# A two-layer transformer on one core: the quantised feed-forward spread over both attentions

## What is computed

```python
x = x + L0_attn(L0_cond(x))          # "layer 0": adapter matmul, 32 small heads
x = x + L0_ffn(L0_cond2(x))          # routed low-rank feed-forward
x = x + L1_attn(L1_cond(x))          # "first attention": 32 heads of 128, 8 kv heads
x = x + L1_ffn(L1_cond2(x))          # "second attention" over 512 cached + 128 own keys,
                                     # then the quantised feed-forward

def _fake_quant_lastdim(x):
    s = jnp.maximum(jnp.max(jnp.abs(x), axis=-1, keepdims=True) / 127.0, 1e-08)
    return jnp.clip(jnp.round(x / s), -127.0, 127.0) * s
def _dyn_quant_linear(x, w, b):
    return jnp.einsum('bti,oi->bto', _fake_quant_lastdim(x), _fake_quant_lastdim(w)) + b
h = _layernorm(vit_embeds, gamma, beta)      # vit_embeds: output of the second attention
h = _dyn_quant_linear(h, w1, b1)             # w1, w3: 512 x 512
h = jax.nn.gelu(h, approximate=False)
h = _dyn_quant_linear(h, w3, b3)
```

## Time and profile before

| | us |
|---|---|
| median of 3 runs (2221.23 to 2223.15) | 2221.28 |
| profiled execution, its own time | 2225.66 |
| its span, first to last instruction | 2223.6 |
| scores of item 60 start at | 2032.69 |
| PE busy | 2057.3 |
| DVE busy | 1564.7 |
| ACT busy | 1304.6 |
| POOL busy | 793.9 |

### The profile page before, as it was taken

How to read it: one execution, slowest core, us unless ns; L and a number is a source line. 1 busy time by engine, 2 the same in 40 slices (tenths; PEclk the granted TensorE clock), 3 DMA queues, 4 the chain that set the end, 5 groups by cost and what they waited for, 6 DMA issues and landing times.

```text
span 2223.6 us, 35355 instructions
## 1 busy us (share of the span) xinstructions
PE 2057.3 (93%) x12261; PEld 1723.7 (78%) x12280; DVE 1564.7 (70%) x3415; ACT 1304.6 (59%) x3765; POOL 793.9 (36%) x779
## 2 busy tenths in 40 slices
PE   6999977999999999989999999999999999999744
PEld 5777656888888888778888888888888888888621
DVE  5566743555555555568878888878788888888787
ACT  3566653544544444456777777767677676777421
POOL 4100004100000000046656666666666666566231
PEclk9999998999999999999999999999999999999955
DMA  8011101001100110121111211111111111121100
GB/s 282 24 49 44 49 1 67 30 23 44 48 29 20 48 48 2 51 71 32 59 50 30 77 33 58 51 32 58 48 57 52 31 59 52 29 67 32 32 10 29
DMA packets 39361, 106.02 MB, mean 48 GB/s; under 512 B 10242, under 2 KB 15618, under 8 KB 34834
## 3 DMA queue, kind: packets, MB, share of 16 engines
q1 hardware_dynamic: 22802, 70.17, 9.0%
q0 software_dynamic: 16384, 33.59, 5.3%
HBM read 101.63 MB, written 2.10 MB: 47 GB/s over the span
## 4 chain that ended last, share of the span: by engine, by line
PE 84%; DVE 10%; ACT 3%; issue 1%; DMA 0%; POOL 0%; SPq 0%; DVEq 0%; ACTq 0%; POOLq 0%
PE PS L1433 9%; PE PS L1445 8%; PE PS L1342 8%; PE PS L1213 7%; PE PS L1273 7%; PE PS L1400 7%; PE PS L1418 6%; PE PS L1356 4%; PE PS L1226 4%; PE PS L1403 3%; PE PS L344 3%; PE PS L1258 2%; PE PS L1241 2%; PE PS L334 2%; PE PS L488 1%
## 5 line engine op out<-in xcount | busy, mean ns | idle before, releaser
L2010 POOL DMA_INDIRECT kcache<-in_kcache,rows x256 | 252.2, 985 | 562.1 <-DVE x_res L1526 491.3
L1662 DVE CUSTOM_DVE_ANT_0 pr<-PS,ffn_weights,sm 128x640 f32<-128x640 f32 x256 | 225.4, 885 | 134.3 <-PE PS L1403 134.3
L2018 POOL DMA_INDIRECT vcache<-in_vcache,rows x256 | 259.4, 1013 | 138.3 <-PE PS L1241 62.7
L1930 ACT ACTIVATE pr<-pr,sm 128x640 f32<-128x640 f32 x256 | 212.8, 831 | 43.7 <-DVE sm L1662 43.7
L1678 DVE TENSOR_TENSOR prT_lo<-PS,prT_hi 128x512 fp32r<-128x512 f32 x320 | 209.6, 686 | 39.7 <-ACT prT_hi L1941 39.1
L1941 ACT ACTIVATE prT_hi<-PS 128x512 fp32r<-128x512 f32 x320 | 178.4, 596 | 67.5 <-PE PS L1418 58.9
L2024 POOL TENSOR_TENSOR vcached_lo<-vcache,vcached_hi 128x512 fp32r<-128x512 f32 x64 | 83.2, 1300 | 276.3 <-ACT vcached_hi L1913 276.3
L1418 PE MATMUL PS<-consts,pr 128*128 128x128 f32 x1280 | 173.6, 273 | 6.9 <-DVE prT_lo L1678 4.6
L1418 PEld LDWEIGHTS PS<-consts,pr 128*128 128x128 f32 x1280 | 150.2, 141 | 32.0 <-DVE prT_lo L1678 6.3
L1803 ACT ACTIVATE pr<-pr,sm 128x128 f32<-128x128 f32 x256 | 99.7, 391 | 105.3 <-DVE sm L1516 103.3
L1400 PE MATMUL PS<-kT_lo,qT_hi 128*128 128x320 f32 x512 | 154.0, 309 | 0.0
(11 more groups left out here) (309 smaller groups left out, 6277.0 us busy)
## 6 DMA issues: line engine op xcount, KB each, us to landing
arena<-in_wqkv SPq DMA_DIRECT2D x16, 1536.0 KB, 6.6
arena<-in_wo SPq DMA_DIRECT2D x16, 1024.0 KB, 5.7
arena<-in_wcT SPq DMA_DIRECT2D x8, 1024.0 KB, 5.8
kcache<-in_kcache,rows POOLq DMA_INDIRECT x256
vcache<-in_vcache,rows POOLq DMA_INDIRECT x256
arena<-in_xT SPq DMA_DIRECT2D x8, 256.0 KB, 6.8
x_res<-in_x SPq DMA_DIRECT2D x1, 2048.0 KB, 14.1
ffn_weights<-in_alibi SPq DMA_DIRECT2D x2, 1024.0 KB, 6.2
```

Source lines behind the costliest of these rows:

```text
L1662: dve.tensor_tensor_reduce(pr2[:, h, :].rearrange("p (a n) -> p a n", a=2), PS[:, SCORE_BANK[h]:SCORE_BANK[h] + 2, 0:HALF], keymask[:, b, ...
L1930: act.activation(pr2[:, h, :], pr2[:, h, :], ACT.Exp, bias=nm2[:, h:h + 1], scale=-1.0, accum_out=rs2[:, h:h + 1]).then_inc(a2_ex, 1)
L2010: pool.indirect_dma_start(out=kcache[:, c, :], out_offset=None, in_=T["kcache"], in_offset=bass.IndirectOffsetOnAxis(ap=rows[:, g, b, c:c ...
L2018: pool.indirect_dma_start(out=vcache[:, c, :], out_offset=None, in_=T["vcache"], in_offset=bass.IndirectOffsetOnAxis(ap=rows[:, g, b, c:c ...
```

## The change

The quantised feed-forward no longer runs behind the second attention.

- **Weights.** The eight 128-row blocks ("units") of w1 and w3 are quantised in the first attention, at items 10, 12, 18, 20, 26, 28, 34 and 36 (`UNIT_ITEM`): DVE takes the row steps in that item and the three passes in the next, PE transposes the block one item later (bank 7), ACT copies it, SP writes it to a DRAM tensor. The steps are written to DRAM as well (in place of the product with a diagonal matrix), and both come back after the last group's weights have left the staging buffers.
- **Rows.** The two linears of sequence b run inside the last group and at its end. With q = i - 56: variance and centring of sequence q-1 (DVE), its root, gamma and beta (POOL); row step, three passes, transposes, linear 1 and its dequantising of sequence q-2; gelu of q-3 (ACT, with one Exp on an idle column behind it); row step, passes, transposes and linear 2 of sequence q-4, scaled by ACT and finished by POOL; the addition to `x_res` of q-5. In the group, all three rounding passes of both linears are on DVE; `quantised_end` has what is left of sequences 3 to 7, and there ACT shares the passes of three of them (`scale_hidden`, `to_bf16`).
- **Form of the passes.** scale and add a magic number; clamp between two bounds; subtract the magic number. The values are the same as before.
- `h16` and `hT16` have one buffer for each linear, both transposes share bank 3, linear 1 writes bank 0 and linear 2 bank 2, and the scores of the next item wait for their readers.

```diff
+            def load_units(first):
+                if first == 0:
+                    sp.wait_ge(a1_xT, B)
+                for n in (first, first + 1):
+                    wait(sp, s_hq, n - 1)
+                    t = n % KT
+                    sp.dma_start(unit_rows[n % 2], T["w3" if n >= KT else "w1"][t * P:(t + 1) * P, :]).then_inc(s_wn, 16)
+
+            def keep_units(first):
+                for n in (first, first + 1):
+                    sp.wait_ge(s_hTc, n + 1)
+                    t = n % KT
+                    sp.dma_start(wT_kept[:, n // KT, :, t * P:(t + 1) * P],
+                                 unit_T16[n % 2].rearrange("p (k n) -> p k n", k=KT)).then_inc(s_wst, 16)
...
+                if 3 <= g < 7:
+                    keep_units(2 * g - 6)
+                if 2 <= g < 6:
+                    load_units(2 * g - 4)
+
+            sp.wait_ge(s_qs, UNITS_Q)
+            sp.dma_start(step_kept.rearrange("(n p) -> p n", p=P), unit_step, allow_slow_non_contiguous=True).then_inc(s_wst, 16)
...
+            sp.wait_ge(s_wst, 16 * (UNITS_Q + 1))
+            sp.dma_start(wT16.rearrange("p w t n -> p (w t n)"),
+                         wT_kept.rearrange("p w t n -> p (w t n)")).then_inc(s_fi, 16)
+            sp.dma_start(wrow.rearrange("p w n -> p (w n)"), step_kept.partition_broadcast(P)).then_inc(s_fi, 16)
...
+        ORDER = [(0, 0), (1, 0)]
+        for _b in range(2, B - 2):
+            ORDER += [(_b - 2, 1), (_b, 0)]
+        ORDER += [(4, 1), (6, 0), (5, 1), (7, 0), (6, 1), (7, 1)]
+        NTH = {bw: n + UNITS_Q for n, bw in enumerate(ORDER)}
...
+            def turn_unit(n):
+                pe.wait_ge(s_hq, n + 1)
+                wait(pe, s_hTc, n)
+                for k in range(KT):
+                    mm = pe.transpose(hbank(7)[:, k * P:(k + 1) * P], unit_q16[n % 2][:, k * P:(k + 1) * P], identb[:])
+                mm.then_inc(s_hT, 1)
...
+                    if h == 0 and i > LAST + 2:
+                        pe.wait_ge(s_dr, i - LAST - 2)
+                    if h == 1 and i > LAST + 2:
+                        pe.wait_ge(s_hTc, NTH[i - LAST - 3, 0] + 1)
+                        wait(pe, s_ev, i - LAST - 4)
...
                 turn_probs(i, 3)
                 turn_probs(i, 4)
+                b = i - LAST
+                if b >= 4:
+                    turn_hidden(b - 4, 1, i)
                 if more:
                     project_q(i + 2, (1, 2, 3) if new_weights else (3,))
+                if b >= 2:
+                    turn_hidden(b - 2, 0, i)
                 weigh(i, 2)
+                if b >= 2:
+                    linear(b - 2, 0, 0, i)
+                if b >= 4:
+                    linear(b - 4, 1, 2, i)
                 weigh(i, 3)
                 weigh(i, 4)
...
+            def linear(b, w, bk, i=None):
+                pe.wait_ge(s_hTc, NTH[b, w] + 1)
+                pe.wait_ge(s_fi, 16 * 6)
+                if i is not None and w == 0:
+                    pe.wait_ge(a2_acc, i)
+                elif i is not None and i + 1 < ITEMS:
+                    pe.wait_ge(a2_kTl, i + 2)
+                for k in range(KT):
+                    mm = pe.matmul(bank(bk), hT16[w][:, k * P:(k + 1) * P], wT16[:, w, k, :],
+                                   start=(k == 0), stop=(k == KT - 1))
+                mm.then_inc(s_lin[w], 1)
...
+                if i in UNIT_ITEM:
+                    unit_steps(UNIT_ITEM.index(i))
+                if i - 1 in UNIT_ITEM:
+                    quantise_unit(UNIT_ITEM.index(i - 1))
...
+            def row_steps(step, inv, rows):
+                ch.link(dve.tensor_reduce(step, rows, AX, ALU.max, apply_absolute_value=True))
+                ch.link(dve.tensor_scalar(step, step, 1.0 / 127.0, 1e-8, ALU.mult, ALU.max))
+                dve.reciprocal(inv, step).then_inc(s_qs, 1)
+
+            def quantise(n, dst, rows, inv):
+                dve.wait_ge(s_qs, n + 1)
+                ch.link(dve.tensor_scalar(rows, rows, inv, MAGIC, ALU.mult, ALU.add))
+                ch.link(dve.tensor_scalar(rows, rows, MAGIC + 127.0, MAGIC - 127.0, ALU.min, ALU.max))
+                dve.tensor_scalar(dst, rows, MAGIC, None, ALU.subtract).then_inc(s_hq, 1)
...
+                q = i - LAST
+                if q >= 4:
+                    hidden_steps(q - 4, 1)
                 for h in range(GH):
...
                 reciprocals(i, (2, 3))
+                if q >= 2:
+                    hidden_steps(q - 2, 0)
                 if i == 0:
...
                     norm_k(i + 1)
+                if q >= 4:
+                    quantise_hidden(q - 4, 1)
                 if i:
...
                     lo_of_own_k(i + 1)
+                if q >= 2:
+                    quantise_hidden(q - 2, 0)
+                if q >= 1:
+                    variance(q - 1)
                 if new_weights:
...
                     lo_of_out_weights(g, 3)
+                if q >= 5:
+                    add_hidden(q - 5)
                 lo_of_probs(i, 4)
...
                     lo_of_weights(g + 1, 4)
+                if q >= 1:
+                    centre(q - 1)
+                if q >= 2:
+                    dequantise1(q - 2, 0)
+
...
+                dve.wait_ge(a2_acc, LAST + b + 1)
+                ch.link(dve.bn_stats(stats[:, b, :], acc2[:, b, :]))
+                ch.link(dve.bn_aggr(mv[:, b, :], stats[:, b, :]))
+                dve.tensor_scalar(qvar[:, b:b + 1], mv[:, b, 1:2], EPS_LN, None, ALU.add).then_inc(s_var, 1)
...
+            def dequantise1(b, bk):
+                n = NTH[b, 0] - UNITS_Q
+                dve.wait_ge(s_lin[0], b + 1)
+                dve.wait_ge(s_fi, 16 * 6)
+                dve.scalar_tensor_tensor(out=acc2[:, b, :], in0=bank(bk), scalar=qstep[:, n:n + 1], in1=wrow[:, 0, :],
+                                         op0=ALU.mult, op1=ALU.mult).then_inc(s_dr, 1)
+                if b >= 6:
+                    dve.wait_ge(s_dr, b + 1)
+                    dve.tensor_tensor(acc2[:, b, :], acc2[:, b, :], brow[:, 0, :], ALU.add).then_inc(s_act, 1)
+
+            def centre(b):
+                dve.wait_ge(s_root, b + 1)
+                return dve.tensor_scalar(acc2[:, b, :], acc2[:, b, :], mv[:, b, 0:1], qrstd[:, b:b + 1], ALU.subtract,
+                                         ALU.mult).then_inc(s_ctr, 1)
...
+            def quantised_end():
+                lo_of_o(ITEMS - 1)
+                hidden_steps(4, 1)
+                hidden_steps(6, 0)
+                clamp(4, 1)
+                clamp(6, 0)
+                add(ITEMS - 1)
+                variance(7)
+                hidden_steps(5, 1)
+                add_hidden(3)
+                normalise_last(7)
+                clamp(5, 1)
+                hidden_steps(7, 0)
+                quantise_hidden(7, 0)
+                dequantise1(6, 7)
+                add_hidden(4)
+                hidden_steps(6, 1)
+                dequantise1(7, 0)
+                quantise_hidden(6, 1)
+                hidden_steps(7, 1)
+                quantise_hidden(7, 1)
+                add_hidden(5)
+                add_hidden(6)
+                dequantise2(7, 7)
...
+                if q >= 4:
+                    hidden_copy(q - 4, 1, upto=NTH[q - 2, 0] + 1)
+                if q >= 2:
+                    hidden_copy(q - 2, 0)
+                if q >= 3:
+                    gelu(q - 3)
                 if after:
                     q_squares(i + 2)
+                if q >= 4:
+                    scale_linear2(q - 4, 2)
+                if q >= 3 and more:
+                    act.activation(idle, qinv[:, 0:1], ACT.Exp)
...
+                q = i - LAST
+                if q >= 1:
+                    layer_norm(q - 1)
+                if q >= 2:
+                    add_bias1(q - 2)
+                if q >= 4:
+                    dequantise2(q - 4)
+            root(7)
+            dequantise2(4)
+            dequantise2(5)
+            dequantise2(6)
```

369 lines of the change are left out of this document (185 added, 184 removed).

## The result

The changed kernel took 2165.51 us (median of four runs, 2163.30 to 2166.13) against 2222.22 us for the kernel before in the same comparison (four runs, 2221.23 to 2225.21): a ratio of 0.9741, 95% interval 0.9724 to 0.9758, or 56.7 us less. The forecast was 2165, with 56.9 less. The profiled execution took 2165.41, span 2163.6.

A forecast was written before the change was run, and what follows sets the result against it. It took PE to bound the kernel up to the end, and DVE the end (the quantised feed-forward). 2.5 + 24.8 + 4.2 + 2.0 - 90.4 = -56.9 us from the median 2221.28 gave 2164.4, stated as 2165; range 2150 to 2179.

The forecast's parts named there:

- Theory A: Last group: DVE and the chain after its last pass set the item period; 2157 to 2173 us, chance 0.55.
- B: Rival: the insertions vanish in slack and PE stays the bound; 2149 us, chance 0.17.
- C: Rival: ACT's table loads or POOL's lateness set the late items' period; 2176 us, chance 0.20.
- The end: After the last weighing: 33.8 us to the end of the span instead of 124.2, so -90.4 us (-94 to -86).
- E: The end of the last weighing, from which the prediction counted the times of the end.
- The cover: First attention: DVE's 1.72 us wait for the exponentials hides the row step (1.10) and passes (1.44), cost 0.
- the ring: Items 60 to 62: DVE's passes end 17.8 us after the scores start; transposes, copies, linears, weighings take 5.0 more.
- POOL wait: Items 61 and 62: DVE waits for POOL's root, due 13.9 us after the scores but wanted at 12.9; +1.0 each.
- The port, +2.0: POOL's new products hold up DVE's scaling of the first two heads and several passes; +2.0 us (0 to 8).
- The upper case: A full block of one POOL product on DVE in each of seven items, about 8 us.
- G: The stretch from the start of item 57's scores to the end of the span.
- D: Rival: not faster, because TensorE falls to 1.2 GHz in the stretched items; 2221 us and above, chance 0.02.

The follow-up runs named there:

- e1_no_clamp: The changed kernel with the middle of the three rounding passes (the clamp) left out: 2156.86 us, ratio 0.9704.
- e5_extra_pass: The changed kernel with the clamp done twice, four rounding passes instead of three: 2171.85 us in one run.
- e3: The changed kernel with POOL's five new operations (gamma, beta, biases, one scale) done on one column only: 2158.63 us, ratio 0.9709.
- e7_tail_dve: The changed kernel with sequence 6's second dequantising in the end on DVE instead of ACT and POOL: 2159.92 us in one run.
- e9_filler: The changed kernel with 22 unread matmuls put into PE's waits of the end: 2165.90 us in one run.

## Why the prediction was right, and where it was not

**The whole.** 56.9 us less were forecast, 56.7 measured; and 2165 against 2165.51. Theory A held: it is shown by the pair of e1_no_clamp and e5_extra_pass, and B and C in both its forms are refuted. That the total fits within a us is luck to a good part: from item 57 on 4.1 us more were gained than forecast, and ahead of it 4.3 us more were lost (6.8 for 2.5).

**The end.** Forecast -90.4, measured 34.38 - 124.17 = -89.8. The step from which this follows, all operations in DVE's written order with the waits put in by hand, held to within 0.6 us as a sum. In detail the clock fell about 4.2 us later than forecast (E+13.2 for E+9; it is worked out from the 0.68 of the window 2141 to 2145, between 1.00 and 0.50 on either side), the dequantising of sequence 7 came at E+19.4 where its linear was forecast to end at E+18.6, and POOL's last products ended at E+28.9 for E+28.3.

**First attention.** Forecast +2.5 (eight sets of transposes at 0.31). The eight items of the units grew by 0.30 us each, 2.4 in sum: right. The cover that I named for DVE's part did hide it. Its wait for the exponentials, on the timeline of DVE in three successive items, with the three passes, with the row step, and with the next unit's passes ahead:

```profile
462.99 0.18 DVE L1650 RECIPROCAL sm<-sm 128x4 f32<-128x4 f32 x1 [0.40 <-ACT pr L2062]
...
472.30 0.18 DVE L1650 RECIPROCAL sm<-sm 128x4 f32<-128x4 f32 x1 [0.74 <-ACT pr L2062]
...
481.89 0.18 DVE L1650 RECIPROCAL sm<-sm 128x4 f32<-128x4 f32 x1 [0.40 <-ACT pr L2062]
```

Of 1.72 us, 0.40 and 0.74 are left, not zero.

**Items 57 to 59.** Forecast 0.5, 2.4 and 2.4; measured 0.38, 2.37 and 2.61.

**Items 60 to 62.** Forecast 5.6, 6.6 and 7.3, in sum 19.5; measured 5.18, 5.42 and 6.32, in sum 16.9. The step that failed is the POOL wait of 1.0 us in 61 and 62. The new products take 1.30 us each where I had 1.4, and V's low half begins 4.5 and 5.2 us after the scores of 61 and 62 where I had 5.5. From its start to the root's end POOL needs 7.9 us, where I had taken 8.4 from the kernel before. So the root was there 12.4 and 13.0 us after the scores, not 13.9, and DVE came for it at 12.6 and 13.2. POOL's chain does end close to DVE's use of it, but 0.16 us ahead and not 1.0 behind. The rest of the ring, 17.8 + 5.0, was right within half a us.

**The port, +2.0.** The contention is there and moved the scaling by 0.1 to 0.9 us an item. The e3 kernel puts all of POOL's length in items 58 to 61 at 1.1 us. For 62 and 63, where the pair grew by 0.93 and 0.87, no run prices it, so the size of the term stays open between about 1 and 3 us. Its place in the sum did not help: the periods above were measured with it and are still shorter than forecast without it, so that something else in them was put too high by as much. The upper case of the prediction, a full product in each of seven items, would be 7 x 1.30 = 9.1 us and not about 8; the trace has nothing of that size.

**Item 63.** Forecast 20.1, measured 20.07; with the same program in e7_tail_dve and e9_filler 19.47 and 19.45, so that the last 0.6 us of the fit is chance.

**The sum of the errors.** For G the forecast was 24.8 + 4.2 + 2.0 - 90.4 = -59.4; measured, 179.09 - 242.56 = -63.5. So 4.1 us more were gained there than forecast: 4.7 less was lost in the items, which is about the absent POOL wait and the port term together, and the end gave 0.6 less. In the profiles item 57 begins 3.5 us later than before, with 2.4 of the units in it. In the medians of the first comparison the gain is 56.7, so that 6.8 us came before item 57, and 4.4 of them are not explained by the new work. The traces show what such a difference can consist of. In the second attention the last item but one of a group (6, 14 and so on to 54), in which PE begins with the next group's weights, takes 20.0 to 20.1 us; but in every profile here one to three of these take 21.3 to 21.5, and these are exactly the ones in which the granted clock falls. Item 22, in the kernel before and in the changed one:

```profile
1358.89:1378.94 20.05, 17.93 (x105) 15.27 (x104) 17.23 (x37) 14.71 (x36) 11.26 (x11) 1.00 0.10 27
...
1361.11:1382.49 21.38, 19.25 (x105) 16.54 (x104) 17.23 (x37) 14.71 (x36) 11.30 (x11) 0.92 0.09 26
```

The profile of the kernel before has one such item (30), that of the changed kernel three (14, 22 and 54): 2.8 us of its later start. The rest of the 3.5 is the units' 2.4, 0.2 between the attentions, and -1.9 from what lies ahead of the first attention, whose first scores start at 336.45 where they started at 338.35. Which items it strikes is not the edits' doing: kernels with the same work there differ in it. That the 4.4 us of the medians are of this kind is argued, not shown, since the runs behind them have no traces.

**D.** The rival of a lower clock in the stretched items did occur, in one item of six and in its mildest form, 0.93. Item 62 is the one in which PE has no projection of a next item to fill its waits, and in other kernels the fall was deeper there (0.86, 0.87); with a fourth pass it came in 60 and 61 as well (0.93). The reason that I gave against D, that item 63 keeps 1.00 with less work, was poor: item 62 has more PE work than item 63 and lost the clock all the same.

## What to carry to other kernels

When work is moved from a serial end into a pipeline with slack, cost it on the engine with the least slack in that pipeline: here each rounding pass on DVE cost its full 0.4 to 0.6 us per item, though DVE was only 80% busy there before, because the added work exceeded its idle time. Cost the ring that starts when the moved work ends (transposes, copy, linear, weighings: 4.75 us), because no busy share shows it. Add a contention or a wait to such a sum only where its margin is worked out to better than its size: the POOL wait was decided by 0.16 us. And before a difference of 1 to 3 us between two profiles is put down to an edit, compare the granted clock of the same stage: the same program gave item 62 at 22.86, 23.56 and 25.17 us.
